# Narrow attention on Trainium2: the first pass of two heads in the two row halves of TensorE, four banks for maxima, three single banks for scores, and a planned order of products

## The chip, the cores and the metric

The kernel is one program on one core of a Trainium2 chip. The metric is the device time of an execution in microseconds (us); lower is better. In the text PE is TensorE, DVE is VectorE, ACT is ScalarE, POOL is GpSimd and SP is SyncE, the engine that issues nearly all DMAs.

## The reference

The reference is a chain of six residual blocks on x of shape (2, 1024, 128): a mixture of experts, a causal attention, a second mixture, a window block (attention and experts), an encoder block with attention, and a second window block. The change touches only the two attentions with 16 heads of dimension 8. The first is causal:

```
q, k, v = jnp.split(x @ W_attn + b_attn, 3, axis=-1)   # 2 batches x 16 heads, 1024 positions, head dim 8
scores = jnp.einsum('bhqd,bhkd->bhqk', q, k) / sqrt(8)
scores = jnp.where(causal, scores, -inf)
o = jnp.einsum('bhqk,bhkd->bhqd', softmax(scores), v)
```

The second, in the encoder block, has no scaling and no mask, and adds a relative bias to the softmax's result before the product with v. In both there are 32 score matrices of 1024 x 1024.

## The kernel before, in words

`narrow_attention` (L1335 to L1614) runs twice: its tiles are named a1x for the causal attention and b1x for the encoder's. Four heads are a group, so there are 8 groups; each group has two halves of 512 queries, so there are 16 halves.

A head has only 8 rows. q and k are each cut into three bf16 parts, and the slots `q_slot` and `k_slot` (three of each, one group per slot) hold on rows 0 to 71 all nine products of parts of q and k; rows 72 to 95 are zero. Three more rows (96 to 98, ones on the side of k) hold minus the row's maximum, again in three parts.

Three kinds of work share PE:

- The **first pass** (L1516) makes scores with queries on the partitions, 96 rows x 128 columns of weights and up to 512 keys, one head at a time into one of three banks `m_bank`. DVE reduces each bank to the row's maximum (L1582). In a1x an item that ends on the diagonal gets a second product (L1519) that adds the mask. After the last item of a half (one more pass over the two parts of the keys and a negation), PE turns the maxima (L1511), DVE copies them to `rest` (L1578), POOL cuts them into parts (L1474 to L1480) and SP copies these to rows 96 to 98 of the slot (L1434).
- The **scores** (L1533) come again with keys on the partitions and all 128 rows, so that they have the maximum taken off. They go into `e_bank`, two banks pairs for two heads each. ACT takes the exponential of two heads at once (L1602, up to 1024 columns) into `probs`. In a1x POOL clears the triangle (L1487).
- The **values** (L1548) are products in fp32, 128 x 32 weights: four heads run beside each other in four column tiles, into `o_bank`. ACT copies `o_bank` at the end of a half (L1614), SP stores it (L1442).

A unit is four heads of one half against 128 keys. b1x has 128 units of 512 queries; a1x has 96 with 128 to 512. The order on PE is fixed when the program is built: for each unit u the scores of unit u+1 and the values of u, and between them the share of first-pass items that `due(u)` gives, in proportion to the columns done. The first pass starts with a lead of `turn_at[AHEAD - 1] + 10` items in a1x, `+ 14` in b1x. So its last item comes shortly before the last units.

The groups are loaded by SP: group 0 in the phase before (`narrow_values` for a1x, `relative_bias` for b1x), groups 1 and 2 as the first thing in `narrow_attention`, and group g (3 to 7) when the last values of group g-3 are done (L1447 to L1455). SP works strictly in order:

```
            narrow.load(sp, 1)
            narrow.load(sp, 2)
            for half in range(AHEAD):
                rows(half)
            for half in range(HALVES):
                group = half // 2 + SLOTS - 1
                if SLOTS <= group < GROUPS and half % 2 == 0:
                    sp.wait_ge(pv_done, last_unit[half - 1] + 1)
                    narrow.load(sp, group)
                if half + AHEAD < HALVES:
                    rows(half + AHEAD)
                store(half)
```

AHEAD is 2 in a1x and 1 in b1x. A load is six DMAs (L1214, L1217) of 192 KB. Each phase (a1w, a1x, b1e, b1x and so on) begins when all engines have finished the one before, SP among them.

## Time and profile before

| | us |
|---|---|
| median of 3 runs (2727.01 to 2735.43) | 2730.46 |
| profiled execution | 2738.76 |
| its span | 2737.0 |
| PE, DVE, ACT, POOL busy | 2467.6, 2083.8, 1427.7, 653.4 |
| a1x: first item of the first pass, start of the last values | 268.2, 544.0 |
| b1x: the same | 1567.6, 1958.1 |

Busy times are sums of the intervals in which an engine had work. A matmul is recorded with its latency, so that two that follow each other overlap: what one costs PE is the distance of two starts, and a PE busy for 90% of the span is not at 90% of its peak. PEld is the load of weights, beside the products. The profile's clock of PE is the share of full speed (2.4 GHz) that was granted.

### The profile page before, as it was taken

The page shows a single profiled execution, that of the slowest core. Times are in us where ns is not written, and L with a number is a line of the kernel's source. Part 1 is how long each engine was busy: PE and PEld are TensorE (multiplying, and loading weights), DVE is VectorE, ACT ScalarE, POOL GpSimd, SP SyncE. Part 2 cuts the span into 40 slices and gives each one's busy share as a digit, 9 for nine tenths or more (in the row PEclk, how much of TensorE's full clock was granted, in tenths as well). Part 3 has the DMA queues.
Part 4 walks back from the last instruction along what each step waited for, and adds up shares of the span by engine and source line. Part 5 has one row for each costly group of instructions (what it writes and reads, how often), then busy time and mean ns, then how long its engine had stood idle before and what let it go on. Part 6 is the DMA issues. An engine that isn't in the chain of part 4 may idle for free. (4 is left out here: it accounts for less than half of the span.)

```text
span 2737.0 us, 39054 instructions
## 1 busy us (share of the span) xinstructions
PE 2467.6 (90%) x12420; PEld 1470.1 (54%) x12420; DVE 2083.8 (76%) x4138; ACT 1427.7 (52%) x3042; POOL 653.4 (24%) x699
## 2 busy tenths in 40 slices
PE   8995999869988999899996599999579899989998
PEld 6773333247756555477774422222136555467776
DVE  4995877439978999289995188888248899639998
ACT  3563455625522787156664046666420577526665
POOL 2324222213335000134445100000005200014443
PEclk9997899979999999899997789999879999989999
DMA  1213011022121000034442601010312000014443
GB/s 67 85 57 90 32 46 41 7 84 82 61 62 28 1 1 1 11 134 150 153 148 48 163 22 39 22 39 5 50 43 47 5 1 1 9 44 146 146 149 119
DMA packets 104852, 166.68 MB, mean 61 GB/s; under 512 B 55170, under 2 KB 77570, under 8 KB 92850
## 3 DMA queue, kind: packets, MB, share of 16 engines
q1 hardware_dynamic: 87812, 162.77, 18.8%
q10 hardware_dynamic: 16896, 2.10, 0.5%
q8 instruction: 77, 1.26, 0.2%
q14 instruction: 67, 0.55, 0.1%
HBM read 145.36 MB, written 12.78 MB: 58 GB/s over the span
## 5 line engine op out<-in xcount | busy, mean ns | idle before, releaser
L1582 DVE TENSOR_REDUCE b1x_maxima<-b1x_m_bank 128x1 f32<-128x512 f32 x512 | 319.2, 682 | 59.4 <-PE b1x_m_bank L1516 58.3
L1602 ACT ACTIVATE b1x_probs<-b1x_e_bank 128x1024 f32<-128x1024 f32 x256 | 248.3, 1021 | 144.1 <-PE b1x_e_bank L1533 144.0
L1582 DVE TENSOR_REDUCE a1x_maxima<-a1x_m_bank 128x1 f32<-128x512 f32 (+3 forms) x384 | 191.3, 548 | 59.3 <-PE a1x_m_bank L1519 30.5
L1602 ACT ACTIVATE a1x_probs<-a1x_e_bank 128x1024 f32<-128x1024 f32 (+1 forms) x192 | 146.2, 812 | 131.7 <-PE a1x_e_bank L1533 131.5
L1516 PE MATMUL b1x_m_bank<-b1a_k_slot,b1a_q_slot 96*128 96x512 bf16 x512 | 186.5, 404 | 12.8 <-DMA b1a_q_slot<-scratch_q_parts 12.6
L1533 PE MATMUL b1x_e_bank<-b1a_q_slot,b1a_k_slot 128*128 128x512 bf16 x512 | 153.5, 383 | 1.7 <-DMA b1a_q_slot<-b1x_max_parts 0.6
L1516 PE MATMUL a1x_m_bank<-a1a_k_slot,a1a_q_slot 96*128 96x512 bf16 (+3 forms) x384 | 121.2, 353 | 20.4 <-POOL a1x_mask L1467 11.6
L1548 PE MATMUL b1x_o_bank<-b1x_probs,b1a_v_aug 128*32 128x512 f32 x1024 | 136.4, 605 | 0.4 <-ACT b1x_probs L1602 0.4
L1516 PEld LDWEIGHTS b1x_m_bank<-b1a_k_slot,b1a_q_slot 96*128 96x128 bf16 x512 | 41.5, 97 | 168.5 <-DVE b1x_maxima L1582 128.9
L687 ACT ACTIVATE g1e_high<-g1e_hidden 128x512 fp32r<-128x512 f32 x128 | 81.0, 633 | 91.5 <-DVE g1e_hidden L718 91.3
L687 ACT ACTIVATE g2e_high<-g2e_hidden 128x512 fp32r<-128x512 f32 x128 | 81.0, 633 | 90.9 <-DVE g2e_hidden L718 90.9
L718 DVE TENSOR_TENSOR g1e_hidden<-g1e_hidden,g1e_share 128x512 f32<-128x512 f32 x128 | 112.9, 882 | 2.7 <-DMA g1e_share<-scratch_combine 1.4
L718 DVE TENSOR_TENSOR g2e_hidden<-g2e_hidden,g2e_share 128x512 f32<-128x512 f32 x128 | 112.9, 882 | 2.4 <-DMA g2e_share<-scratch_combine 1.2
L634 PE MATMUL g1e_gate_up<-g_h_high,g_w_high 128*128 128x512 f32 x256 | 100.5, 393 | 1.3 <-DVE g1e_hidden L711 1.3
L634 PE MATMUL g2e_gate_up<-g_h_high,g_w_high 128*128 128x512 f32 x256 | 100.5, 393 | 1.0 <-DVE g2e_hidden L711 1.0
L360 POOL TENSOR_TENSOR g_down_low<-g_w_down,g_down_high 128x128 fp32r<-128x128 f32 x64 | 48.5, 758 | 216.1 <-ACT g_down_high L681 216.1
L634 PE MATMUL g2e_gate_up<-g_h_low,g_w_high 128*128 128x512 f32 x256 | 99.8, 390 | 0.0
L634 PE MATMUL g1e_gate_up<-g_h_low,g_w_high 128*128 128x512 f32 x256 | 99.7, 390 | 0.0
L634 PE MATMUL g1e_gate_up<-g_h_high,g_w_low 128*128 128x512 f32 x256 | 99.7, 389 | 0.0
L634 PE MATMUL g2e_gate_up<-g_h_high,g_w_low 128*128 128x512 f32 x256 | 99.7, 389 | 0.0
L1516 PEld LDWEIGHTS a1x_m_bank<-a1a_k_slot,a1a_q_slot 96*128 96x128 bf16 x384 | 35.9, 98 | 114.4 <-DVE a1x_maxima L1582 81.6
L1533 PE MATMUL a1x_e_bank<-a1a_q_slot,a1a_k_slot 128*128 128x512 bf16 (+3 forms) x384 | 93.5, 329 | 2.9 <-ACT a1x_probs L1602 1.9
(574 smaller groups left out, 6650.7 us busy)
## 6 DMA issues: line engine op xcount, KB each, us to landing
g1e_share<-scratch_combine SPq DMA_DIRECT2D x32, 1024.0 KB, 4.8
g2e_share<-scratch_combine SPq DMA_DIRECT2D x32, 1024.0 KB, 4.8
f1e_share<-scratch_combine SPq DMA_DIRECT2D x9, 1024.0 KB, 4.9
f2e_share<-scratch_combine SPq DMA_DIRECT2D x9, 1024.0 KB, 4.8
g_w<-in_win_experts SPq DMA_DIRECT2D x64, 128.0 KB, 4.5
b1e_window<-scratch_bias_table SPq DMA_DIRECT2D x16, 320.0 KB, 4.9
f_w<-in_moe_w SPq DMA_DIRECT2D x18, 256.0 KB, 4.9
a1a_k_slot<-scratch_k_parts SPq DMA_DIRECT2D x24, 192.0 KB
```

The source lines that it names most:

```text
L360: pool.tensor_tensor(self.down_low[slot][:], self.w_down[slot][:], self.down_high[slot][:], ALU.subtract).then_inc(self.down_low_done, 1)
L634: mm = pe.matmul(gate_up[j % 2][:, which, :], a[slot][:, at], b[:, chunk(n)], start=(part == 0), stop=(part == 2))
L687: act.activation(high[j % SLOTS][:], hidden[j % SLOTS][:], ACT.Copy).then_inc(high_done, 1)
L718: dve.tensor_tensor(hidden[s][:], hidden[s][:], share[slot][:, chunk(n)], ALU.mult).then_inc(hidden_done, 1)
L1516: mm = pe.matmul(bank[:, 0:width], q_slot[s][0:MAX_ROW, qt // 4, hh, chunk(qt % 4, 128)], k_slot[s][0:MAX_ROW, hh, k0:k0 + width], start=T ...
L1533: mm = pe.matmul(e_bank[pair][:, a, 0:width], k_slot[s][:, hh, chunk(kt, 128)], q_slot[s][:, qh, hh, lo - qh * NC:], start=True, stop=True)
L1548: mm = pe.matmul(o_bank[32 * hh:32 * hh + 32, at:at + width], v_aug[:, half // 2, kt, chunk(hh, 32)], probs[u % 2][:, hh, 0:width], start= ...
L1582: dve.tensor_reduce(maxima[:, k0 // NC, col:col + 1], bank[:, 0:width], AX, ALU.max).then_inc(m_taken, 1)
L1602: act.activation(probs[u % 2][:, 2 * pair:2 * pair + 2, 0:width], e_bank[pair][:, :, 0:width], ACT.Exp, scale=scale).then_inc(exp_done, 1)
```

## The change

The first pass now takes two heads per item. The even head's product uses rows 0 to 63 of the slots; the odd head's uses rows 64 to 127 of two new tiles, `q_odd` and `k_odd`, that SP fills by copies of rows 0 to 63 of the odd heads from the slots. The products left out of the first pass are those on rows 64 to 71 (third part of q with third part of k). Each item fills two of four `m_bank`; DVE still reduces each with one instruction. In a1x the mask is still added with a product of 128 rows, one for each head.

The scores have three single banks, one head each, and ACT takes one exponential per head (up to 512 columns). PE's order is now the answer of `order_of_products`, which plays through the work with constants for the costs and takes at each step what can begin first. It lets the first pass run up to three groups ahead. SP issues the maxima's three rows one by one as POOL has them, and the copies of the odd heads at the places shown.

```diff
         self.q_slot = [phase.sb(f"q_slot{s}", [128, 2, 4, NC], BF16) for s in range(3)]
         self.k_slot = [phase.sb(f"k_slot{s}", [128, 4, L], BF16) for s in range(3)]
+        self.q_odd = [phase.sb(f"q_odd{s}", [128, 2, 2, NC], BF16) for s in range(3)]
+        self.k_odd = [phase.sb(f"k_odd{s}", [128, 2, L], BF16) for s in range(3)]
         self.v_aug = phase.sb("v_aug", [128, GROUPS, GRANULE_TILES, 128])
...
+    def copy_odd(self, sp, group):
+        s = group % SLOTS
+        sp.wait_ge(self.slot_loaded[s], 16 * LOADS * (group // SLOTS + 1))
+        sp.dma_start(self.k_odd[s][64:128, :, :], self.k_slot[s][0:64, 1::2, :]).then_inc(self.odd_loaded[s], 16)
+        sp.dma_start(self.q_odd[s][64:128, :, :, :].rearrange("r e h q -> r (e h) q"),
+                     self.q_slot[s][0:64, :, :, :].rearrange("r e h q -> r (e h) q")[:, 1::2, :]
+                     ).then_inc(self.odd_loaded[s], 16)
...
+def order_of_products(units, items, first_bank, last_item, causal):
+    SIGNAL, SWITCH, READY, CHAIN = 0.1, 0.09, 0.2, 3.6
+    kept = dict(pe=0.0, dve=0.0, act=0.0, kind=None)
+    taken, turned, rows, exps, valued, copied = [], {}, {}, [], [], {}
+    to_score, to_value, scores_to_value = [], [], []
+    m = g = u = 0
+    def begin(kind, since):
+        return max(kept["pe"], since) + (SWITCH if kept["kind"] not in (None, kind) else 0.0)
+    def item_begin():
+        if m == len(items) or items[m][0] >= (units[u][0] // 2 + SLOTS) * 2:
+            return None
+        half, qt = items[m][0:2]
+        since = taken[first_bank[m + 1] - M_BANKS - 1] + SIGNAL if first_bank[m + 1] > M_BANKS else 0.0
+        if qt is None:
+            return begin("fp32", max(since, turned[half] + SIGNAL))
+        return begin("rows", since)
+    def score_begin():
+        of = g // 4
+        if of == len(units) or of > u + 1:
+            return None
+        half, since = units[of][0], exps[g - E_BANKS] + SIGNAL if g >= E_BANKS else 0.0
+        if g % 4 == 0 and (of == 0 or units[of - 1][0] != half):
+            if half not in rows:
+                return None
+            since = max(since, rows[half])
+        return begin("full", since)
+    def value_begin():
+        if g < 4 * u + 4:
+            return None
+        half, kt, lo, width = units[u]
+        since = exps[4 * u + 3] + SIGNAL + (0.5 if causal and lo == kt * 128 else 0.0)
+        if half > 0 and units[u - 1][0] != half:
+            since = max(since, copied[half - 1] + SIGNAL)
+        return begin("fp32", since)
+    while u < len(units):
+        choices = [(at + bias, kind, at) for at, kind, bias in
+                   [(item_begin(), "item", 0.1 if causal else 0.0), (score_begin(), "score", 0.1 if causal else 0.0),
+                    (value_begin(), "value", 0.3)] if at is not None]
+        _, kind, at = min(choices)
+        if kind == "item":
+            half, qt = items[m][0:2]
+            if qt is None:
+                kept.update(pe=at + 0.06, kind="fp32", dve=max(kept["dve"], at + 0.06 + READY) + 0.27)
+                taken.append(kept["dve"] + 0.06)
+                rows[half] = kept["dve"] + CHAIN
+            else:
+                width = items[m][4]
+                end, last = at + width / 2400 + 0.004, "rows"
+                if causal and items[m][3] + width == (qt + 1) * 128:
+                    end, last = end + SWITCH + 0.114, "full"
+                kept.update(pe=end, kind=last)
+                for _ in range(2):
+                    kept["dve"] = max(kept["dve"], end + READY) + width / 960 + 0.066
+                    taken.append(kept["dve"] + 0.07)
+                if m == last_item[half]:
+                    kept["dve"] += 0.35
+                    turned[half] = kept["dve"]
+            m += 1
+        elif kind == "score":
+            width = units[g // 4][3]
+            kept.update(pe=at + width / 2400 + 0.004, kind="full")
+            since = max(kept["act"], kept["pe"] + READY)
+            if g % 4 == 0 and g // 4 >= 2:
+                since = max(since, valued[g // 4 - 2] + SIGNAL)
+            kept["act"] = since + width / 1400 + 0.19
+            exps.append(kept["act"] + 0.1)
+            to_score.append(m)
+            g += 1
+        else:
+            half, kt, lo, width = units[u]
+            kept.update(pe=at + width / 592, kind="fp32")
+            valued.append(kept["pe"])
+            to_value.append(m)
+            scores_to_value.append(g)
+            if u + 1 == len(units) or units[u + 1][0] != half:
+                kept["act"] = max(kept["act"], kept["pe"] + READY) + 0.55
+                copied[half] = kept["act"] + 0.07
+            u += 1
+    return to_score, to_value, scores_to_value
 def narrow_attention(nc, tag, sbuf, dram, narrow, causal):
...
     last_item = [max(m for m, item in enumerate(items) if item[0] == half) for half in range(HALVES)]
     for half in reversed(range(HALVES)):
-        items.insert(min(last_item[half] + 4, len(items)), (half, None))
+        items.insert(min(last_item[half] + 3, len(items)), (half, None))
     turn_at = [items.index((half, None)) for half in range(HALVES)]
     first_item = [min(m for m, item in enumerate(items) if item[0] == half) for half in range(HALVES)]
     last_item = [max(m for m, item in enumerate(items) if item[0] == half and item[1] is not None)
...
-        cut_after.append(during + 1 if late else during)
+    scored = [sum(1 for n in items_to_score if n <= turn_at[half]) for half in range(HALVES)]
+    cut_after = [n // 4 - 1 for n in scored]
     with Phase(nc, tag) as p:
-        m_bank = [p.ps(f"m_bank{s}") for s in range(3)]
-        e_bank = [p.ps(f"e_bank{s}", [128, 2, NC]) for s in range(2)]
+        m_bank = [p.ps(f"m_bank{s}") for s in range(M_BANKS)]
+        e_bank = [p.ps(f"e_bank{s}") for s in range(E_BANKS)]
         o_bank = p.ps("o_bank")
         q_slot, k_slot, v_aug = narrow.q_slot, narrow.k_slot, narrow.v_aug
+        q_odd, k_odd = narrow.q_odd, narrow.k_odd
         probs = [p.sb(f"probs{s}", [128, 4, NC]) for s in range(2)]
         o_sb = [p.sb(f"o_sb{s}", [128, NC]) for s in range(2)]
         maxima = p.sb("maxima", [128, 2, 32])
...
@@ -1429,8 +1525,8 @@
             def rows(half):
                 s, qh = (half // 2) % SLOTS, half % 2
-                sp.wait_ge(cut, 4 * half + 4)
                 for i in range(PARTS):
+                    sp.wait_ge(cut, 4 * half + (1, 3, 4)[i])
                     sp.dma_start(q_slot[s][MAX_ROW + i:MAX_ROW + i + 1, qh, :, :],
                                  max_parts[qh][:, i, :]).then_inc(rows_set[qh], 16)
@@ -1444,6 +1540,8 @@
             narrow.load(sp, 1)
             narrow.load(sp, 2)
+            narrow.copy_odd(sp, 1)
+            narrow.copy_odd(sp, 2)
             for half in range(AHEAD):
                 rows(half)
             for half in range(HALVES):
@@ -1453,6 +1551,8 @@
                     narrow.load(sp, group)
                 if half + AHEAD < HALVES:
                     rows(half + AHEAD)
+                if SLOTS <= group < GROUPS and half % 2 == 0:
+                    narrow.copy_odd(sp, group)
                 store(half)
             for s in range(2):
                 sp.wait_ge(o_stored[s], 64 * GROUPS)
...
@@ -1501,38 +1601,43 @@
             def first_pass(m):
                 half, qt = items[m][0:2]
-                bank, s = m_bank[m % 3], (half // 2) % SLOTS
+                s, b = (half // 2) % SLOTS, first_bank[m]
                 if half % 2 == 0 and m == first_item[half]:
                     pe.wait_ge(slot_loaded[s], 16 * LOADS * (half // 2 // SLOTS + 1))
-                if m >= 3:
-                    pe.wait_ge(m_taken, m - 2)
+                    pe.wait_ge(narrow.odd_loaded[s], 32 * (half // 2 // SLOTS + 1))
+                if first_bank[m + 1] > M_BANKS:
+                    pe.wait_ge(m_taken, first_bank[m + 1] - M_BANKS)
                 if qt is None:
                     pe.wait_ge(neg_done, half + 1)
-                    pe.transpose(bank[0:16, 0:128], neg_max[:, half % 2, :],
+                    pe.transpose(m_bank[b % M_BANKS][0:16, 0:128], neg_max[:, half % 2, :],
                                  sbuf["ident"][:]).then_inc(m_done, 1)
                     return
                 hh, k0, width = items[m][2:]
                 diagonal = causal and k0 + width == (qt + 1) * 128
-                mm = pe.matmul(bank[:, 0:width], q_slot[s][0:MAX_ROW, qt // 4, hh, chunk(qt % 4, 128)],
-                               k_slot[s][0:MAX_ROW, hh, k0:k0 + width], start=True, stop=not diagonal)
+                even = pe.matmul(m_bank[b % M_BANKS][:, 0:width], q_slot[s][0:64, qt // 4, hh, chunk(qt % 4, 128)],
+                                 k_slot[s][0:64, hh, k0:k0 + width], start=True, stop=not diagonal)
+                odd = pe.matmul(m_bank[(b + 1) % M_BANKS][:, 0:width],
+                                q_odd[s][64:128, qt // 4, hh // 2, chunk(qt % 4, 128)],
+                                k_odd[s][64:128, hh // 2, k0:k0 + width], start=True, stop=not diagonal)
                 if diagonal:
-                    mm = pe.matmul(bank[:, width - 128:width], ident_bf[:], mask[:, 0, :],
-                                   start=False, stop=True)
-                mm.then_inc(m_done, 1)
-            def scores(u, pair):
+                    even = pe.matmul(m_bank[b % M_BANKS][:, width - 128:width], ident_bf[:], mask[:, 0, :],
+                                     start=False, stop=True)
+                    odd = pe.matmul(m_bank[(b + 1) % M_BANKS][:, width - 128:width], ident_bf[:],
+                                    mask[:, 0, :], start=False, stop=True)
+                even.then_inc(m_done, 1)
+                odd.then_inc(m_done, 1)
+            def scores(g):
+                u, hh = g // 4, g % 4
                 half, kt, lo, width = units[u]
                 s, qh = (half // 2) % SLOTS, half % 2
-                if pair == 0 and (u == 0 or units[u - 1][0] != half):
-                    pe.wait_ge(rows_set[qh], 48 * (half // 2) + 48)
-                if u >= 1:
-                    pe.wait_ge(exp_done, 2 * u - 1 + pair)
-                for a in range(2):
-                    hh = 2 * pair + a
-                    mm = pe.matmul(e_bank[pair][:, a, 0:width], k_slot[s][:, hh, chunk(kt, 128)],
-                                   q_slot[s][:, qh, hh, lo - qh * NC:], start=True, stop=True)
-                mm.then_inc(e_done, 1)
+                if hh == 0 and (u == 0 or units[u - 1][0] != half):
+                    pe.wait_ge(rows_set[qh], ROWS * (half // 2 + 1))
+                if g >= E_BANKS:
+                    pe.wait_ge(exp_done, g - E_BANKS + 1)
+                pe.matmul(e_bank[g % E_BANKS][:, 0:width], k_slot[s][:, hh, chunk(kt, 128)],
+                          q_slot[s][:, qh, hh, lo - qh * NC:], start=True, stop=True).then_inc(e_done, 1)
             def values(u):
...
@@ -1550,40 +1655,40 @@
                                    start=first, stop=last, skip_group_check=True)
                 mm.then_inc(pv_done, 1)
-            for m in range(dues[0]):
-                first_pass(m)
-            for pair in range(2):
-                scores(0, pair)
+            m = g = 0
             for u in range(NU):
-                share = list(range(dues[u], dues[u + 1]))
-                for pair in range(2):
-                    if u + 1 < NU:
-                        scores(u + 1, pair)
-                    if pair < len(share):
-                        first_pass(share[pair])
+                while g < scores_to_value[u]:
+                    while m < items_to_score[g]:
+                        first_pass(m)
+                        m += 1
+                    scores(g)
+                    g += 1
+                while m < items_to_value[u]:
+                    first_pass(m)
+                    m += 1
                 values(u)
-                for m in share[2:]:
-                    first_pass(m)
         @block.vector
...
         def _(act):
-            def exponentials(u):
+            def exponential(g):
+                u, hh = g // 4, g % 4
                 width = units[u][3]
-                if u >= 2:
+                if u >= 2 and hh == 0:
                     act.wait_ge(pv_done, u - 1)
-                for pair in range(2):
-                    act.wait_ge(e_done, 2 * u + pair + 1)
-                    act.activation(probs[u % 2][:, 2 * pair:2 * pair + 2, 0:width],
-                                   e_bank[pair][:, :, 0:width], ACT.Exp, scale=scale).then_inc(exp_done, 1)
-            exponentials(0)
+                act.wait_ge(e_done, g + 1)
...
                 half = units[u][0]
-                if u + 1 < NU:
-                    exponentials(u + 1)
+                while g < scores_to_value[u]:
+                    exponential(g)
+                    g += 1
                 if u == last_unit[half]:
                     act.wait_ge(pv_done, u + 1)
                     if half >= 2:
...
@@ -1627,6 +1733,7 @@
         def _(sp):
             sp.wait_ge(narrow.stored, 16 * narrow.stores)
             narrow.load(sp, 0)
+            narrow.copy_odd(sp, 0)
         @block.gpsimd
         def _(pool):
```

## Rows read from the trace of the kernel before

**Rows 1.** Stages: length, busy us (count) of PE PEld DVE ACT POOL, PEclk, DMA share, GB/s.
```profile
296.00:515.00 219.00, 206.43 (x1526) 78.53 (x1525) 169.76 (x358) 130.94 (x177) 60.97 (x160) 0.99 0.12 33
1568.00:1595.00 27.00, 26.38 (x47) 4.65 (x45) 26.75 (x47) 0.00 (x0) 1.40 (x4) 0.50 0.23 75
1596.00:1933.00 337.00, 335.90 (x1877) 99.05 (x1875) 296.61 (x509) 233.91 (x249) 19.53 (x56) 0.99 0.08 22
1933.00:1960.00 27.00, 23.46 (x139) 4.53 (x139) 1.11 (x4) 22.28 (x24) 1.40 (x4) 1.00 0.02 4
```

**Rows 2.** First pass, scores, values: duration min/median/max ns; first and last start us.
```profile
L1516 PE MATMUL b1x_m_bank<-b1a_k_slot,b1a_q_slot x512: 379/379/634, 1567.6 to 1932.0; 96*128 96x512 bf16 x171
...
L1533 PE MATMUL b1x_e_bank<-b1a_q_slot,b1a_k_slot x512: 377/379/634, 1596.2 to 1955.9; 128*128 128x512 bf16 x171
...
L1533 PE MATMUL a1x_e_bank<-a1a_q_slot,a1a_k_slot x384: 217/377/634, 296.5 to 542.3; 128*128 128x512 bf16 x96, 128*128 128x384 bf16 x32, 128*128 128x256 bf16 x32, 128*128 128x128 bf16 x32
...
L1548 PE MATMUL b1x_o_bank<-b1x_probs,b1a_v_aug x1024: 592/605/617, 1600.6 to 1958.1; 128*32 128x512 f32 x171
...
L1548 PE MATMUL a1x_o_bank<-a1x_probs,a1a_v_aug x768: 269/550/617, 300.4 to 544.0; 128*32 128x512 f32 x96, 128*32 128x384 f32 x32, 128*32 128x256 f32 x32, 128*32 128x128 f32 x32
```

**Rows 3.** Timeline of PE in b1x, one unit: start us, us, instruction, count.
```profile
1703.43 0.59 PE L1533 MATMUL b1x_e_bank<-b1a_q_slot,b1a_k_slot 128*128 128x512 bf16 x2
1703.87 0.38 PE L1516 MATMUL b1x_m_bank<-b1a_k_slot,b1a_q_slot 96*128 96x512 bf16 x1
1704.17 1.07 PE L1548 MATMUL b1x_o_bank<-b1x_probs,b1a_v_aug 128*32 128x512 f32 x8
1705.17 0.39 PE L1516 MATMUL b1x_m_bank<-b1a_k_slot,b1a_q_slot 96*128 96x512 bf16 x1
```

**Rows 4.** Timeline of DVE in b1x; idle before in brackets.
```profile
1699.93 2.48 DVE L1582 TENSOR_REDUCE b1x_maxima<-b1x_m_bank 128x1 f32<-128x512 f32 x4 [0.35 <-PE b1x_m_bank L1516]
```

**Rows 5.** Reductions of a1x by form: busy us, mean ns, idle before.
```profile
L1582 DVE TENSOR_REDUCE a1x_maxima<-a1x_m_bank 128x1 f32<-128x512 f32 x192 | 122.4, 683 | 41.1 <-PE a1x_m_bank L1516 27.0 <-PE a1x_m_bank L1519 13.9
...
L1582 DVE TENSOR_REDUCE a1x_maxima<-a1x_m_bank 128x1 f32<-128x128 f32 x64 | 15.9, 279 | 13.7 <-PE a1x_m_bank L1519 13.5
```

**Rows 6.** Timeline of ACT near the end of a1x.
```profile
541.12 1.09 ACT L1602 ACTIVATE a1x_probs<-a1x_e_bank 128x512 f32<-128x512 f32 x2 [0.38 <-PE a1x_e_bank L1533]
```

**Rows 7.** Timeline of PE in the window attention: products in row halves (L920).
```profile
999.62 0.59 PE L915 MATMUL g1a_scores<-g1a_mask,g1a_ident_bf 128*128 128x512 bf16 x2
1000.15 1.13 PE L920 MATMUL g1a_scores<-g1s_k,g1s_q 64*128 64x256 f32 x8
1001.21 1.08 PE L944 MATMUL g1a_outs<-g1a_probs_T,g1s_v 128*64 128x512 f32 x4
```

**Rows 8.** DMA rate around the first loads of b1x, then of a1x.
```profile
1562.00:1590.00 28.00, 0.50 0.28 88
...
1590.00:1592.00 2.00, 0.50 0.07 29
...
286.00:288.00 2.00, 0.50 0.08 32
```

**Rows 9.** One load in mid-course: SP's issue, and the DMA rate.
```profile
333.47 0.32 SPq L1214 DMA_DIRECT2D a1a_k_slot<-scratch_k_parts  x1
...
332.00:346.00 14.00, 1.00 0.31 93
...
346.00:348.00 2.00, 1.00 0.07 26
```

**Rows 10.** Timeline of SP and ACT where b1x begins.
```profile
1550.43 0.33 SPq L1214 DMA_DIRECT2D b1a_k_slot<-scratch_k_parts  x1
...
1556.54 1.28 ACT L1602 ACT_TABLE_LOAD   x1 [1.24 <-PEq L47]
```

**Rows 11.** Timeline of SP where a1x begins.
```profile
250.32 0.35 SPq L1214 DMA_DIRECT2D a1a_k_slot<-scratch_k_parts  x1
...
258.56 0.37 SPq L1428 DMA_DIRECT2D a1x_mask_f<-in_causal_mask  x1
```

51 lines of the change are left out of this document (24 added, 27 removed).

## Prediction

> **What bounds the kernel now.** I read the stages first. In b1x, from the first score to the last first-pass product, PE is busy 335.9 of 337 us, DVE 296.6, ACT 233.9 [rows 1]; in the same stretch of a1x PE has 206.4 of 219. So PE bounds both. The timeline of PE shows what a unit costs. From 1703.43 two products of 512 columns take 0.44, so 0.213 each at the full clock; the last first-pass product starts 0.30 before the values, 0.09 more than its columns; the values start 1.00 before the next product [rows 3]. A unit of b1x is thus 8 x 0.213 + 0.09 + 1.00 = 2.80 us of PE without a gap. DVE takes four reductions in 2.48 the last with its 0.68 [rows 4, 5], so 0.60 each, 2.40 per unit, and sat idle 0.35 for PE before them.
>
> Second come the ends. The first score of b1x starts at 1596.2, 28.6 after the first first-pass product, and the last values at 1958.1 (they last to 1958.7); in a1x 296.5 and 544.0, with 0.4 more [rows 2]. Third, the DMAs. Loads of groups 0 to 2 keep the DMA engines at 88 GB/s until about 1591 in b1x, and end at 287 in a1x [rows 8]. A lone load, issued at 333.47, runs at 93 GB/s until 347 [rows 9]: 13.5 us for 1.18 MB.
>
> I have the new order from the listing of the planner, followed by its rules; I take from it only which product stands where, no time. Its result: b1x has 22 pairs before the first score, then units such as R SSS R S V and R SSS R S R V (R a pair, S a score, V values), the last pair in unit 96 of 128, and 593 changes between pairs, full products (128 rows) and fp32 products (values, turned maxima), 129 of them away from fp32. a1x has 15 pairs before the first score, the last turned maxima in unit 73 of 96, and 500 changes, 104 away from fp32. In both, 31 and some 23 units stand behind the end of the first pass.
>
> **Pairs in row halves.** The trace has such products in the window attention. Behind two 512-column products begun at 999.62 (0.43) they start at 1000.15, 0.10 late; four heads of 256 columns then take 1.06 until the next kind [rows 7]. That is 512 columns side by side at the price of a values block (1.00) and 0.05 to start the second half. So a pair costs 0.213 + 0.05, and each change of kind 0.095 (0.09 and 0.10), the one behind fp32 being in the 1.00. The Trainium skill (TensorEngine Tiling, Key Properties) says that changing the tiling mode drains TensorE, with no price; by it alone the sum would lack a term, and the trace's 0.09 and 0.10 supply it. A bf16 pair is not shown: it might start with no delay (0) or need the 0.15 that values take to leave per change; I take 0.095, from neighbouring bf16 rows.
>
> PE work from the first score on, in b1x: scores 512 x 0.213 = 109; values 128; pairs (256 - 22) x 0.263 = 62; changes 464 x 0.095 = 44; turned maxima 1: 344 us. Before: 109 + 128 + (512 - 46) x 0.213 = 99, changes 128 x 0.09 = 12, 1: 349. Halving the first pass saves 49 and gives 44 back, because a pair mostly stands alone between scores. In a1x all scores have 147,456 columns per pass: scores 61.4; values the same + 96 x 0.15 = 75.8; pairs 137,700 columns left / 4800 = 28.7 + 177 x 0.05 = 8.9; masks 236 x 128 columns = 12.5; 386 changes 36.7 (each diagonal item has one of its own, before its masks); 1: 225. Before: 61.4 + 75.8 + 53.3 + 11 + 1 + 96 x 0.09 = 211. So +14.
>
> **DVE and the order.** DVE's instructions stay; four banks let it run without PE's 0.35. b1x: 468 reductions after the first score x 0.60 = 281, and 16 x 0.6 for the small ones of a half (three instructions, each the size of a 128-column reduction's 0.20): 290. Behind it stand 31 units without a first pass. ACT needs for one of those 4 x 0.49 (two of 512 columns in 1.09, the last 0.60 [rows 6]) = 1.98, PE 1.95, with the copy out 2.04: 63. DVE's bound is 353, PE's 344. Before, only 14 units stood there (27 us [rows 1]). The run-ahead spends what the banks bring. a1x: reductions 0.60 for 512 columns and 0.20 for 128 (their means less the 0.08 of overlap), 0.47 and 0.33 between [rows 5], = 180 in all, 175 with the small ones left, and 43 behind: 218, under PE's 225.
>
> **ACT.** 512 exponentials of 0.49 are 253 against 256 x 0.94 = 241 before (233.9 for 249 [rows 1]), beside a PE of 344: nothing, unless PE fell below 260. Three single banks hold 1.5 us of its work, more than a values block; no stall taken (0 to 0.2 us per unit, 25 in all, if the return of a bank is late).
>
> **The start.** SP now waits for group 0 in the phase before, which can't end without it. b1x: the load is issued at 1550.43 [rows 10]; 13.5 us make 1564, then two issues of copies, the bias stores, and the change of phase: b1x begins at 1567.5, not 1556.5. The copy (0.5 MB on 64 rows) is in no row: at least the 0.7 of its two issues (0.33 [rows 10]), at most 0.5 MB at 88 GB/s and 2 for the way, 8; I take 5, nearer to the slow rate, since 64 rows spread wider than 24. First pair 1569.5 (was 1567.56, so +2). But groups 1 and 2 are issued 11 us later, and SP waits for both (`copy_odd(1)`, `copy_odd(2)`) before `rows(0)`, without which no score starts. 2.36 MB at 88 GB/s is 27, with copies and bias 30: landed 1597.5, copies issued, rows landed by 1602.5. First score 1602.5, +6.3. The 22 pairs need 44 x 0.60 = 26.4 and are done. a1x: load issued 250.3, landed 264, begins 266.5 instead of 258.56 [rows 11]; groups 1 and 2 landed 296, first score 301, +4.5, with only 15 pairs done where 62 of 400 items were. PE's clock is 0.50 in such a lead now [rows 1] and I expect it so again.
>
> **Loads in mid-course.** A load starts when the values of group g-3 are done; SP then needs 13.5 + 0.5 + 5 = 19 us before the first pair of group g may run, and PE waits in order. By the plan that pair stands, in b1x, many units behind the load for groups 3 to 6, but only units 80 to 83 lie between for group 7: 10 pairs, 12 us of DVE and as much of PE. Stall 7. In a1x group 5 has units 36 to 40: 20 scores of some 380 columns 3.2, five values 3.7, 11 pairs 2.5, six pairs of masks 0.6, some 26 changes 2.5, so 13 us. By the same count group 6 has units 48 to 51 (9) and group 7 units 60 and 61 (6): stalls 6, 10, 13, sum 29; groups 3 and 4 have 19 or more. Bounds: with a copy of 0.7 each stall is 4 less, 17 and 3; with 8, 38 and 10. Behind the waiting PE stand the scores, so ACT and DVE run dry. `copy_odd` also stands before `store(half)`: no cost, o_sb has two buffers. The three rows issued one by one shorten a chain on which nothing waits once the first pass is three halves ahead: 0.
>
> **Sum.** b1x before: 362.5 from first score to end, of which 349 work, 13 gaps. After: 344 + 7 + gaps of 8 = 359 by PE, and 353 + 6 = 359 by DVE; two bounds so near cost each other some 5: 364, from 1602.5 to 1966.5, +8. a1x before: 248 = 211 + 37 gaps. After: 225 + 29 + 12 (more banks, and stalls in which the others catch up), from 301 to 567, +22. Together +30: 2739 + 30 = 2769 for the profiled execution, which lay 8 above the median; on the median 2730.5 + 30 = 2761.
>
> **Rivals.**
> *Loads hidden.* If the copies cost next to nothing and the loads land early, scores start at 1594.5 and 285, and no stall comes: b1x 1594.5 + 353 = 1947.5 (-11), a1x 285 + 225 + 12 = 522 (-22). 2697. For it: PE bounds, and DVE gets its banks. Against: 13.5 us per load stands in the rows. It decides for faster from where the stalls are below about 6 us in all. 0.09.
> *Stalls absorbed.* First scores as forecast, but the units between load and use run longer than I count, so that no stall is left: b1x 1602.5 + 353 = 1955.5 (-3), a1x 301 + 225 + 12 = 538 (-6), 2721 (2706 to 2736). Against: five short units can't last 19 us. 0.12.
> *Pairing at full worth.* Changes and second starts cost nothing: b1x stays at DVE's bound with its stall, 1961.5 (+3), a1x 301 + 218 + 29 = 548 (+4): 2737, no difference. Against: the 0.09 and 0.10. The same page (Theoretical Speedup) gives up to 2x for 64 rows or less, and (PSUM Bottleneck) no faster evacuation; the trace agrees on the side-by-side run. 0.07.
> *Changes dearer.* 0.15 each as behind fp32: 850 x 0.055 = 47 more, 2808. 0.08. *Loads worse* (copies at 8): 2773 and more. 0.04. The rest, 0.60, is the forecast (2735 to 2785).
>
> Faster by over 0.3% (8 us, what can be told from no change): 0.09 + 0.08 = 0.17. Within: 0.11, from the pairing case, half of the absorbed one and the forecast's edge. Slower 0.72. Range 2712 to 2790.
>
> **What would show it.** The wait of PE for `odd_loaded` or the loads at the first item of groups 5 to 7 in a1x (6 to 13 us each) and group 7 in b1x (7); first scores 4 to 7 us later from the phase's old clock; the last reduction of b1x some 60 us before its end; reductions 0.60 apart; pairs in 0.26; b1x with PE busy throughout in spite of fewer columns. Wrong if a score starts before slot 2 has landed, if the waits are under 2 us, or if a unit of b1x takes under 2.7 with two pairs in it.

## The result, and the profile after

The changed kernel takes 2803.5 us (median; 2797.1 to 2816.5), the one before, beside it, 2732.9: 1.025 times as long [1.0217, 1.0281]. Forecast were 2761 (+30) and a range of 2712 to 2790; measured were +70, outside it. The direction was right, the size not. The profiled execution took 2805.24 us, its span 2803.5, 66.5 more than before.

Stages of the kernel after, as in [rows 1]: length, busy us (count) of PE, PEld, DVE, ACT and POOL, granted clock, DMA share, GB/s. They run from the first score to the last reduction and from there to the last values, in a1x and in b1x; the last line is mid-course of b1x.

```profile
297.90:543.50 245.60, 201.86 (x1482) 65.39 (x1482) 178.86 (x388) 129.54 (x308) 58.52 (x155) 0.88 0.16 40
543.50:592.10 48.60, 39.56 (x276) 10.61 (x273) 1.35 (x5) 37.23 (x92) 12.99 (x33) 1.00 0.03 6
1646.70:1952.50 305.80, 291.14 (x1650) 69.34 (x1651) 287.86 (x510) 209.86 (x404) 19.48 (x56) 0.98 0.13 32
1952.50:2023.40 70.90, 64.98 (x373) 14.06 (x369) 1.26 (x5) 63.63 (x124) 1.39 (x4) 1.00 0.02 4
...
1700.00:1740.00 40.00, 39.69 (x233) 9.49 (x225) 39.68 (x71) 28.18 (x56) 2.78 (x8) 1.00 0.19 47
```

Mid-course of b1x DVE is busy 39.68 of 40 us where PE waited for nothing; in [rows 1] it had 0.88 of its stretch. The pairs do feed it. But a1x has PE idle for 44 of 246 us, and in b1x DVE is finished 70.9 us before the last values.

Where the lines begin and end in the kernel after, as in [rows 2] (L1617 even half of a pair, L1639 score, L1653 values, L1687 reduction).

```profile
L1617 PE MATMUL a1x_m_bank<-a1a_k_slot,a1a_q_slot x192: 212/386/607, 269.8 to 541.9; 64*128 64x512 bf16 x96, 64*128 64x128 bf16 x32, 64*128 64x256 bf16 x32, 64*128 64x384 bf16 x32
...
L1639 PE MATMUL b1x_e_bank<-b1a_q_slot,b1a_k_slot x512: 377/389/634, 1646.7 to 2021.8; 128*128 128x512 bf16 x171
...
L1653 PE MATMUL a1x_o_bank<-a1x_probs,a1a_v_aug x768: 269/592/1026, 303.6 to 592.1; 128*32 128x512 f32 x96, 128*32 128x384 f32 x32, 128*32 128x256 f32 x32, 128*32 128x128 f32 x32
...
L1653 PE MATMUL b1x_o_bank<-b1x_probs,b1a_v_aug x1024: 592/617/1063, 1652.3 to 2023.4; 128*32 128x512 f32 x171
...
L1687 DVE TENSOR_REDUCE b1x_maxima<-b1x_m_bank x512: 669/681/693, 1615.2 to 1952.5; 128x1 f32<-128x512 f32 x171
```

a1x ends 48.1 us later than before (592.1 against 544.0). b1x ends 65.3 later (2023.4 against 1958.1), of which 44.5 was there when its load was issued (1594.95 against 1550.43), so its own share is 20.8. The two make the 66.5, but for 2.4 of scatter in the stages between and behind (the profiled executions below scatter by up to 9 us ahead of a1x as well, in stages that no edit touches; so stretches are compared inside a1x and b1x).

PE's four long waits in mid-course, each in front of the first pair of a group (timeline; in brackets the idle time and what ended it, "issue" where the profile names nothing; there too the copy of the odd heads had landed 0.09 us before):

```profile
429.35 0.26 PE L1617 MATMUL a1x_m_bank<-a1a_k_slot,a1a_q_slot 64*128 64x128 bf16 x1 [8.40 <-issue]
469.87 0.26 PE L1617 MATMUL a1x_m_bank<-a1a_k_slot,a1a_q_slot 64*128 64x128 bf16 x1 [12.04 <-issue]
514.44 0.26 PE L1617 MATMUL a1x_m_bank<-a1a_k_slot,a1a_q_slot 64*128 64x128 bf16 x1 [15.50 <-DMA a1a_q_odd<-a1a_q_slot]
1910.35 0.58 PE L1617 MATMUL b1x_m_bank<-b1a_k_slot,b1a_q_slot 64*128 64x512 bf16 x1 [10.39 <-DMA b1a_q_odd<-b1a_q_slot]
```

What SP did ahead of the third of them: the load, then the copies of the odd heads.

```profile
496.12 0.32 SPq L1217 DMA_DIRECT2D a1a_k_slot<-scratch_k_parts  x1
...
509.93 0.67 SPq L1229 DMA_DIRECT2D a1a_k_odd<-a1a_k_slot  x1
510.65 0.64 SPq L1230 DMA_DIRECT2D a1a_q_odd<-a1a_q_slot  x1
```

And what the clock does behind the waits:

```profile
429.40:433.40 4.00, 4.00 (x21) 1.45 (x21) 1.54 (x7) 2.17 (x4) 0.78 (x3) 0.54 0.02 6
514.50:518.50 4.00, 4.00 (x28) 1.62 (x29) 1.26 (x5) 1.82 (x6) 0.82 (x3) 0.51 0.00 0
1910.40:1914.40 4.00, 4.00 (x15) 0.75 (x16) 1.75 (x3) 0.60 (x1) 0.00 (x0) 0.50 0.02 4
```

From the load's issue to PE's return are 18.3 us, 13.8 to the copy's issue and 4.5 for the copy. Then PE runs at 1.2 GHz for some 4 us, though it was at 2.4 before the wait.

One unit of b1x, the one of [rows 3]. Both halves of a pair now begin together, here 0.32 before the scores:

```profile
1703.40 0.39 PE L1617 MATMUL b1x_m_bank<-b1a_k_slot,b1a_q_slot 64*128 64x512 bf16 x1
1703.40 0.39 PE L1619 MATMUL b1x_m_bank<-b1a_k_odd,b1a_q_odd 64*128 64x512 bf16 x1
1703.72 0.82 PE L1639 MATMUL b1x_e_bank<-b1a_q_slot,b1a_k_slot 128*128 128x512 bf16 x3
1704.48 0.39 PE L1617 MATMUL b1x_m_bank<-b1a_k_slot,b1a_q_slot 64*128 64x512 bf16 x1
...
1705.69 1.07 PE L1653 MATMUL b1x_o_bank<-b1x_probs,b1a_v_aug 128*32 128x512 f32 x8
1706.69 0.39 PE L1617 MATMUL b1x_m_bank<-b1a_k_slot,b1a_q_slot 64*128 64x512 bf16 x1
```

The pair costs 0.32 = 0.213 + 0.11 for the change behind it, three scores 0.76 = 3 x 0.213 + 0.12 for the next. Alone between scores a pair costs 0.213 + 0.11 + 0.12 = 0.44; the two 96-row products that it replaces cost 2 x 0.213 = 0.43. So a pair between scores gains nothing. One that stands directly behind the values is another matter: the values start 1.00 before it, as they did before the 96-row product, so its change in is not paid again, and its 0.32 stand against 0.43. What that makes in all was to be tested.

### The profile page after: what moved, and what is told of

It is laid out like the page before. It is cut to its first block and busy times, and to the rows that moved or that the text cites. A ratio compares the mean times of both kernels' runs of the same rounds, so it can differ in the third digit from the quotient of the medians.

```text
span 2803.5 us, 39540 instructions
## 1 busy us (share of the span) xinstructions
PE 2444.0 (87%) x12420; PEld 1431.5 (51%) x12420; DVE 2070.2 (74%) x4138; ACT 1460.2 (52%) x3490; POOL 652.9 (23%) x699
## 5 line engine op out<-in xcount | busy, mean ns | idle before, releaser
L1687 DVE TENSOR_REDUCE b1x_maxima<-b1x_m_bank 128x1 f32<-128x512 f32 x512 | 309.2, 676 | 44.3 <-PE b1x_m_bank L1619 44.1
L1707 ACT ACTIVATE b1x_probs<-b1x_e_bank 128x512 f32<-128x512 f32 x512 | 264.8, 604 | 132.3 <-PE b1x_e_bank L1639 130.0
L1687 DVE TENSOR_REDUCE a1x_maxima<-a1x_m_bank 128x1 f32<-128x512 f32 (+3 forms) x384 | 187.1, 550 | 92.2 <-PE a1x_m_bank L1623 83.7
L1707 ACT ACTIVATE a1x_probs<-a1x_e_bank 128x512 f32<-128x512 f32 (+3 forms) x384 | 160.2, 499 | 141.7 <-PE a1x_e_bank L1639 140.9
L1639 PE MATMUL b1x_e_bank<-b1a_q_slot,b1a_k_slot 128*128 128x512 bf16 x512 | 157.0, 388 | 11.4 <-DMA b1a_q_slot<-b1x_max_parts 6.3
L1617 PE MATMUL b1x_m_bank<-b1a_k_slot,b1a_q_slot 64*128 64x512 bf16 x256 | 104.5, 409 | 41.4 <-POOL b1x_ident_bf L1564 15.1
L1653 PE MATMUL b1x_o_bank<-b1x_probs,b1a_v_aug 128*32 128x512 f32 x1024 | 137.3, 608 | 0.7 <-ACT b1x_probs L1707 0.7
L1639 PE MATMUL a1x_e_bank<-a1a_q_slot,a1a_k_slot 128*128 128x512 bf16 (+3 forms) x384 | 101.5, 345 | 22.5 <-DMA a1a_q_slot<-a1x_max_parts 14.7
L1617 PEld LDWEIGHTS b1x_m_bank<-b1a_k_slot,b1a_q_slot 64*128 64x128 bf16 x256 | 23.8, 93 | 184.1 <-DVE b1x_maxima L1687 139.7
L1617 PE MATMUL a1x_m_bank<-a1a_k_slot,a1a_q_slot 64*128 64x512 bf16 (+2 forms) x192 | 67.4, 356 | 55.2 <-issue 21.0
L1619 PE MATMUL b1x_m_bank<-b1a_k_odd,b1a_q_odd 64*128 64x512 bf16 x256 | 104.6, 410 | 0.0
```

The lines of the kernel that those rows point to most:

```text
L1617: even = pe.matmul(m_bank[b % M_BANKS][:, 0:width], q_slot[s][0:64, qt // 4, hh, chunk(qt % 4, 128)], k_slot[s][0:64, hh, k0:k0 + width], ...
L1619: odd = pe.matmul(m_bank[(b + 1) % M_BANKS][:, 0:width], q_odd[s][64:128, qt // 4, hh // 2, chunk(qt % 4, 128)], k_odd[s][64:128, hh // 2, ...
L1639: pe.matmul(e_bank[g % E_BANKS][:, 0:width], k_slot[s][:, hh, chunk(kt, 128)], q_slot[s][:, qh, hh, lo - qh * NC:], start=True, stop=True) ...
L1653: mm = pe.matmul(o_bank[32 * hh:32 * hh + 32, at:at + width], v_aug[:, half // 2, kt, chunk(hh, 32)], probs[u % 2][:, hh, 0:width], start= ...
L1687: dve.tensor_reduce(maxima[:, k0 // NC, col:col + 1], m_bank[(b + odd) % M_BANKS][:, 0:width], AX, ALU.max).then_inc(m_taken, 1)
L1707: act.activation(probs[u % 2][:, hh, 0:width], e_bank[g % E_BANKS][:, 0:width], ACT.Exp, scale=scale).then_inc(exp_done, 1)
```

## The experiments

Ratios are to the kernel before, with 95% intervals; "after" is the changed kernel (2803.5), from which each starts unless another is named. The kernel before was run again beside every series (medians 2732.9 to 2741.3), so between series the ratios compare better than the times.

**The run-ahead.** With the values in group g, the planner lets the first pass go on to group g + 2 (three groups, if that of the values is counted). The load of that group is issued only when the values of group g - 1 are done. With SLOTS - 1 it stops at group g + 1; this is called the lead of two groups below.

```
-        if m == len(items) or items[m][0] >= (units[u][0] // 2 + SLOTS) * 2:
+        if m == len(items) or items[m][0] >= (units[u][0] // 2 + SLOTS - 1) * 2:
```

> The changed kernel, with the first pass allowed at most one group ahead of the values' group (SLOTS - 1 in item_begin). By the new order each load then has at least 8 units more before its first pair; the last turned maxima stand in unit 110 (b1x) and 81 (a1x) instead of 97 and 73. Theory A (the waits for loads in mid-course and the half clock behind each are the main cost): the waits of 8.4, 12.0 and 15.5 us in a1x and 10.4 and 2.0 in b1x are gone, with about 2 us for each of four spells of half clock: 56 us less, and some 5 more from the shorter tails; about 2745. Theory B (the waits only move idle time that DVE and ACT need anyway): under 20 us less, 2785 or more.

2743.0, ratio 1.0038 [1.0015, 1.0061]: theory A. No wait of PE above 1.2 us is left in mid-course, only those at the starts, and the last reduction of b1x is 43 us before its end, not 71. One constant of the planner is worth 60 of the 70 us. From first score to end a1x is 45.6 us shorter and b1x 15.3.

**The start.** `rows(0)` moves ahead of `copy_odd(1)`, `rows(1)` ahead of `copy_odd(2)`.

> The changed kernel, with the rows of half 0 issued by SP before the copies of groups 1 and 2 (the rows of half 1, in a1x, between the two). Theory A (SP's waits for groups 1 and 2 hold up the first score): first score of a1x 10 to 14 us earlier, of b1x 6, PE's two waits for max_parts (14.3 and 6.3) gone; 15 to 20 us less in all. Theory B (the first pass of group 1 waits for its copy anyway): under 6 less.

2793.1, 1.0197 [1.0166, 1.0228]. First pair to first score falls from 28.1 to 24.0 us in a1x and from 32.2 to 28.0 in b1x; the mid-course waits stay (8.16, 12.00, 15.08). This lies between the theories: SP's order was in the way, but it was worth 8 us in the trace (10 by the medians, with intervals that overlap), not 15 to 20, and a1x's first score came 4 us earlier, not 10 to 14.

**Row halves and copies.** First both heads as products of 96 rows from the slots, copies kept; then the copies and their waits out as well.

```
-                even = pe.matmul(..., q_slot[s][0:64, qt // 4, hh, ...], k_slot[s][0:64, hh, ...], ...)
-                odd = pe.matmul(..., q_odd[s][64:128, ...], k_odd[s][64:128, ...], ...)
+                even = pe.matmul(..., q_slot[s][0:MAX_ROW, qt // 4, hh, ...], k_slot[s][0:MAX_ROW, hh, ...], ...)
+                odd = pe.matmul(..., q_slot[s][0:MAX_ROW, qt // 4, hh + 1, ...], k_slot[s][0:MAX_ROW, hh + 1, ...], ...)
```

> The changed kernel, in which both heads of a pair are multiplied from the slots with 96 rows, one after the other; order, banks, copies and all waits stay. Theory A (a pair in row halves costs 0.21 + 0.10 for the way out and 0.10 for the way in against 0.43, so it gives PE next to nothing): 5 to 20 us more than the changed kernel. Theory B (pairing halves the first pass in full): 60 to 85 us more.

> As the one before, and the copies of the odd heads with all their waits (on SP and PE) are gone. Theory A (the copies cost time by what waits behind them): against the kernel with copies, each mid-course wait is 4 to 5 us shorter (three in a1x, one in b1x), the first scores come 6 (b1x) and 10 to 13 us (a1x) earlier and b1x begins 9 us earlier: 35 to 50 us less in all, so about 2765 to 2780. Theory B (the loads alone make the waits): under 15 less.

2811.4, 1.0275 [1.0251, 1.0299]: 8 more than after, with intervals that overlap; in the traces first score to end grows by 8.6 us in b1x and 2.5 in a1x. And 2774.7, 1.0139 [1.0112, 1.0165]: 37 less than that. So the halves are worth some 8 us and their copies cost 37; theory A both times. The traces split the 37: from load to first score a1x falls from 47.7 to 39.4 us and b1x from 52.6 to 42.9, 18 together; the waits in mid-course fall from 45 to 27 (3.43, 7.27, 10.82 and 5.62 without copies), 18 more.

With the lead of two groups the same two edits give:

> The changed kernel with the lead of at most one group, products of 96 rows, no copies and no waits for them: what is left of the change is the banks and the planned order. Theory A (row halves are worth nothing net): equal to the kernel with the lead alone within 10 us, 2733 to 2750. Theory B (with the waits gone PE bounds again, and pairing shows its worth): 15 us or more slower than that, over 2758.

2744.0, 1.0026 [1.0001, 1.005], the same as with halves and copies (1.0038): theory A. But the edit takes out two things, and the traces show that each had its worth. From first score to end of b1x, the first run and then this one, with the same counts of products:

```profile
1597.33:1959.28 361.95, 347.30 (x1980) 82.37 (x2017) 289.81 (x513) 272.03 (x527) 20.88 (x60) 0.99 0.11 28
1581.62:1955.74 374.12, 364.32 (x1980) 103.58 (x2017) 293.79 (x515) 272.09 (x527) 20.94 (x60) 1.00 0.07 20
```

The halves save 12.2 us of b1x (1.4 of a1x). The copies cost 16.6 us ahead of the first scores: from load to first score a1x takes 47.4 us with them and 39.3 without, b1x 52.1 and 43.7. The two hide each other in the total. Where the 12 come from, by the medians of start to start in b1x: a pair behind the values lasts 0.32 against 0.44 of two full products, one between scores 0.39 against 0.48, one ahead of the values 0.32 against 0.53; but three scores ahead of a pair last 0.75 against 0.65. So a pair gains 0.10 to 0.12 beside the values and nothing between scores.

**The copies put into the kernel before**, its products left as they are:

> The kernel before, with the copies of the odd heads and all their waits on SP and PE added, the products unchanged (nothing reads the copies). Theory A (SP's waits at the start are a cost of their own, and in mid-course the old order leaves room for them): first scores 5 us later in b1x and up to 5 in a1x, no wait at later groups; 8 to 18 us slower than before. Theory B (the copies are free under the old lead, and only the run-ahead made them dear): under 5.

2746.3, 1.003 [1.0008, 1.0052]: 8 us by the ratio, 5 by the medians, between the theories. From load to first score b1x takes 6.2 us longer and a1x 2.6; PE waits for a copy once, 1.36 us for group 1 of a1x, and at no later group. So the copies cost a few us by themselves, at the start, and only the run-ahead made them dear in mid-course.

**The banks.** `M_BANKS, E_BANKS = 3, 4`.

> The changed kernel with three banks for maxima and four for scores instead of four and three; the planner's order follows from it: the first pass can't run far ahead (its last item at unit 120 of b1x and 88 of a1x, each group's first pair 16 or more units behind its load), 463 and 478 changes of kind instead of 593 and 500. Theory A (mid-course waits, the half clock behind them and the long end with three score banks make most of the loss): no such waits, ends of 8 units in place of 31; about 2735 to 2750, like the run with the shorter lead. Theory B (DVE needs the fourth bank for a pair while it reduces the other): b1x falls to PE and DVE in turn, 2.9 us a unit or more, and the time stays above 2765.

2871.5, 1.0488 [1.0454, 1.0521], the slowest of all: theory B. A pair takes two of three banks, so that the next has to wait for a reduction (71 such waits of PE in b1x, 61 us): mid-course of b1x both engines are then far from full.

```profile
1750.00:1790.00 40.00, 30.07 (x157) 6.86 (x156) 30.69 (x53) 18.86 (x37) 2.79 (x8) 0.81 0.16 43
```

**The clock.** Products of no use (34, 50 and 66 in a1x, 44 in b1x) fill PE's waits for the loads.

> The changed kernel, with products of 512 columns that nothing reads in PE's four long waits of mid-course (34, 50 and 66 in a1x, 44 in b1x; 7 to 14 us each at full clock, a little less than each wait), in a bank that is free. Theory A (an idle PE loses the clock, and what follows runs 4 us at half of it, 2 us lost each time): the clock stays at 1.00 through the waits and the kernel is 6 to 10 us faster than the changed one. Theory B (the clock behind a wait costs nothing, since DVE and ACT bound the restart): 0 to 2 us.

2799.8, 1.022 [1.0181, 1.0259], 4 less than after, within the intervals and between the theories. The filled stretch keeps its clock:

```profile
428.00:434.00 6.00, 5.94 (x45) 2.12 (x47) 4.69 (x14) 3.95 (x8) 1.40 (x4) 1.00 0.01 2
```

a1x is 5.1 us shorter (317.5 from its first pair against 322.6), b1x 0.7. So the clock behind the waits is a tenth of the 60 us.

**The first copy moved into the phase,** with the lead of two groups. SP issues load 1, copy 0, load 2, rows 0, copies 1 and 2.

> The changed kernel with the lead of at most one group, and a start in which the phase before no longer waits: SP issues the load of group 1, the copy of group 0, the load of group 2, the rows of half 0, then the copies of groups 1 and 2 (in a1x the rows of half 1 between them). Theory A (SP's order of waits at the start costs its 10 to 16 us whatever the order of the products): 10 to 16 us under the run with the lead alone, about 2730. Theory B (the first copy, now beside the loads, lands so late that the first pass loses what the scores win): within 4 us of it.

2759.2, 1.0069 [1.0031, 1.0107], 16 more than the lead alone (8 by the ratios): worse than either theory. The copy stands behind the load of group 1 and beside that of group 2, and the first pair waits for it:

```profile
281.77 0.26 PE L1619 MATMUL a1x_m_bank<-a1a_k_slot,a1a_q_slot 64*128 64x128 bf16 x1 [25.35 <-DMA a1a_q_odd<-a1a_q_slot]
1587.90 0.58 PE L1619 MATMUL b1x_m_bank<-b1a_k_slot,b1a_q_slot 64*128 64x512 bf16 x1 [29.78 <-DMA b1a_q_odd<-b1a_q_slot]
```

Issued at 1569.18, it landed at 1587.9: 18.7 us for what takes 4.5 alone.

**The order.** The kernel before's rule (each unit gets its share of the first pass) in place of the planner; then the same with the pairs of a unit side by side (SSS RR S V) and the start of the second run; then that order with 96-row products and neither copies nor that start.

> The changed kernel with pairs, copies and banks as they are, but with the order of before: each unit takes its share of the first pass in proportion, two scores, a pair, two scores, the other pairs, the values; the lead is half of that of before, in pairs. Theory A (the run-ahead is the main loss, and a pair between scores is worth 0.1 us of a unit's 2.8): no mid-course waits, a unit of 2.7 us in b1x; 2730 to 2745, 55 to 70 under the changed kernel. Theory B (the planned order was worth something by itself): 10 us or more above the planned order with the lead of one group (2743), so over 2753.

> As the one before, with all pairs of a unit together between the third and the fourth score (SSS RR S V), and the rows of half 0 sent before the copies of groups 1 and 2. Theory A (what a pair costs is mostly the two changes of kind around it, so two in one visit save 0.1 to 0.2 us per unit): a unit of 2.6 us in b1x, b1x some 20 us and a1x 10 shorter than in the kernel before, start and copies 8 longer: 2705 to 2720, faster than both kernels. Theory B (DVE, which then gets its four banks in one go, is left idle between visits): no better than 2735.

> As the one before, with 96-row products in place of the row halves, and without copies and their waits: a unit is 8 x 0.213 + 0.09 + 1.00 = 2.80 us again. Theory A (in this order the row halves do pay, for here one pair of changes serves two pairs): 2725 to 2745, 10 to 30 slower than with row halves. Theory B (DVE sets the pace in this order): equal within 5 us, or faster by the start it does not pay.

2756.2, 1.0064 [1.0041, 1.0087]; 2754.0, 1.0062 [1.0038, 1.0086]; 2770.5, 1.0116 [1.0085, 1.0147]. The first is theory B: the planned order was worth something, 3 us of a1x and 6 of b1x in the traces. The second is theory B by its time; pairs side by side shorten b1x by 9.1 us from first score to end (367.8 to 358.7), but a1x takes 13.7 more (251.7 to 265.5), which I can't explain. The third is 16 us slower than the second, as theory A has it, though both lie higher than forecast: without halves b1x takes 373.6 from first score to end, 14.9 more, and a1x 263.6, no more at all. So side by side the halves are worth 15 us of b1x, where they were worth 12 in the planned order. In b1x such a unit takes 2.62 us, but one per half gets a third pair and takes 4.16, PE waiting for DVE:

```profile
1731.24 0.39 PE L1637 MATMUL b1x_m_bank<-b1a_k_slot,b1a_q_slot 64*128 64x512 bf16 x1 [1.03 <-DVE b1x_maxima L1707]
```

**Both repairs**, and then both with units of exactly two pairs in b1x:

> Lead of two groups (as in the first experiment) and the first rows ahead of the copies of groups 1 and 2 (as in the second), together. The first alone came to 1.0038 of before (2743), the second took 10 us off the changed kernel. Theory A (two causes, each its own stretch of time: the loads in mid-course, the first rows at the start): the gains add, 2743 - 10 = 2733, ratio 1.000; in the trace no wait of over 2 us of TensorE inside either pass, and none for the first rows. Theory B (with the lead of one group gone, the vector engine sets the end of both passes, so products that start earlier only end in a longer tail): 2740 to 2743, ratio 1.003, with the first scores 10 us earlier and the last reductions where the first experiment has them.

> As the run before it, and in the full-length pass (the second one) the order is by units of exactly SSS RR S V: three scores, two pairs, a score, the values; the transposition is worth nothing in the due times, so no unit gets a third pair. In the run with pairs together a unit of this kind took 2.62 us and the one unit per half with three pairs 4.16, 22.6 us per half. Theory A (the unit with a third pair was the loss): 8 units of 2.62 and the transposition 0.5 make 21.5 us per half, 16 halves 344 and the same start and tail: the pass is 18 to 22 us shorter than the planned order, so 2710 to 2716, ratio 0.99 to 0.994, faster than before. Theory B (the vector engine needs its 64 reductions and the maxima work of each half all the same, 23 us at 0.60 each and nothing left over in 20 us windows, so the order can't go below it): the pass stays within 5 us of the planned order's, 2732 to 2740; the vector engine's busy share is over 0.98 in the course of it.

2737.5, 1.0001 [0.9982, 1.0019]: the repairs add, though PE still waits for the first rows (9.9 us in a1x, 1.5 in b1x) where none was expected. And 2730.0, 0.9981 [0.9961, 1.0]: at the edge of a gain, far from theory A's 0.99. In both PE is nearer to full than DVE in mid-course of b1x (first the run with the planner's order, then with two pairs a unit):

```profile
1750.00:1790.00 40.00, 39.11 (x225) 9.10 (x224) 33.90 (x62) 30.16 (x60) 2.78 (x8) 1.00 0.17 40
```

```profile
1750.00:1790.00 40.00, 38.76 (x236) 9.27 (x229) 36.55 (x65) 30.43 (x59) 2.79 (x8) 1.00 0.20 48
```

A half takes 22.2 us in the latter, by 13 intervals of its turned maxima, not 21.5, and 21.9 in the former. PE waits some 0.6 us in front of each turned maxima, until DVE has emptied a bank; that makes most of the difference to the 21.5. Theory B's pass came, within 5 us of the planned one, but not by its reason: DVE was busy 0.91, not 0.98. b1x as a whole is 3 us shorter, and the rest of the 7.5 us between the medians lies in stages that the edit does not touch, so I don't claim it. No version was found that is clearly faster than the kernel before.

## Why the prediction was right in kind and wrong in size

**Right.** The start of b1x: from the load's issue to the first score 51.8 us against 45.8, +6.0 where +6.3 was forecast; slot 2 landed and its copies were issued before the rows, as worked out. The mid-course waits stand where they were forecast (groups 5, 6, 7 in a1x, 7 in b1x), ended by the copy, with 18.2 to 18.7 us from load to pair (forecast 19) and 4.5 for the copy (5). DVE sets b1x until its reductions end: 305.8 with waits of 12.4, forecast 290 and 7. The halves' worth: 49 saved and 44 given back were forecast for b1x, so 5 net, and their removal cost it 8.6 us (12.2 with the lead of two groups). The total did not show this, 1.0038 and 1.0026, since the copies at the starts cost as much. The Trainium skill (TensorEngine Tiling, Key Properties) has the change of tiling mode drain TensorE and gives no price; the trace has 0.11 to 0.12, where I had taken 0.095, but the half beside it starts 0.00 to 0.01 later, not 0.05: a lone pair 0.44, forecast 0.45.

**Mis-sized, b1x (+8 forecast, +20.8 measured).** From first score to end 377.2, forecast 364. *Stall 7*: 10.39 and a lesser one of 2.04, +5. *The end at 63*: 70.6, +7.6. Its 31 units take 2.28 each where ACT's 4 x 0.49 and its copies gave 2.04, and ACT is busy 63.63 of 70.90. With four single score banks (the run with 3 and 4 banks) a unit at the end takes 1.97. So this is the stall of three single banks that I bounded at 25 us and took at none.

**Mis-sized, a1x (+22 forecast, +48 measured)**: the larger failure. From first score to end 294.5, forecast 266, though the first score came only 1.4 late (4.5 forecast). *Stalls 6 + 10 + 13 = 29*: 8.40 + 12.04 + 15.50 = 36, +7. From the issue of these loads (410.61, 451.69, 496.12) PE had 10.3, 6.1 and 2.8 us of work left, where I counted 13, 9 and 6 (in b1x 8.2 for 12); why it went faster than counted is not shown. *Gaps of 12, since more banks and the stalls let the others catch up*: besides the three waits PE is idle 245.6 + 48.6 - 201.9 - 39.6 - 35.9 = 17, +5. *Work of 225*: busy 241, +16. The first run shows how this divides: without stalls a1x takes 248.9 from first score (288.9) to end (537.8), 12 more than my 225 + 12, so the work and gaps of the order as such were counted too low by 12. They are what the kernel before had (248). The stalls take the other 45.6: 36 in themselves, about 5 by the clock behind them (the run with fillers), where I expected 0.50 only in the lead, and some 5 that I can't place; the order of the first run differs also by a shorter end (30.4 us behind the last reduction, not 47.9).

**What the range left out.** The bounds moved the stalls with the copy's price alone. What sets them is the run-ahead, and it acts three times: by the waits, by their clock, and by the longer end on an ACT with three banks. This is the step that failed most: I priced one of the three, the waits, and took the other two at nothing. The second is a1x's work and gaps without any stall, 225 + 12, where the runs without stalls have 249. The terms are not independent; removed together by one constant they were 60 us, while the waits as such were 46.

The rival of absorbed stalls (2721) is what the first run tested. Without stalls the kernel stands at 2743: b1x takes 362.0 from first score to end, not 353, and a1x 248.9, not 237. Both are the lengths of before (362.5 and 248). In b1x PE is busy 38.4 to 39.5 of 40 us in such runs and DVE, from 1700 us on, 34 to 37, so that PE, with its changes, stays the bound. That b1x is no longer and no shorter than before is a balance: without halves and copies the same order takes 374.1, 12 more than the kernel before, and the halves take 12 back.

## What to carry to other kernels

Before halving products by rows, count the changes of kind in the order as it will run. At 0.11 us each, a 512-column pair between full products returns nothing; one behind an fp32 product, or two side by side, gain some 0.1 us each. Test the halves apart from the copies that feed them: one total that stood still held a gain of 12 us and a cost of 17. A run-ahead that is allowed up to the number of slots reaches products whose load has not been issued long enough; keep it one slot short, and count load and copy together. A wait in mid-course costs more than its length, since the clock and the buffers behind it have to be paid too.

## What the runs showed of the hardware

- Two products of 64 rows in the two row halves start 0.00 to 0.01 us apart and run side by side (0.39 both).
- Between a pair and full bf16 products a change took 0.11 us on the way out and 0.10 to 0.12 on the way in. Behind fp32 values (1.00 us to the next start) a pair came no later than a 96-row product.
- With three single score banks and nothing but scores and values left, a unit took 2.28 us on average; with four, 1.97.
- PE's granted clock, 1.00 before, was 0.50 to 0.54 for 4 us behind waits of 8.4 to 15.5 us.
- A copy of 0.5 MB from SBUF to SBUF took 4.5 us alone, and 18.7 behind and beside two loads of 1.18 MB.
